# Two token halves, or two phases: the gated feed-forward of a fused two-layer kernel

## The reference

```python
def _binary_diff_weight(w, base):
    d = w - base
    coeff = jnp.mean(jnp.abs(d))
    return base + coeff * jnp.sign(d)
W1 = _binary_diff_weight(w1, mean_w1)     # (1792, 512)
W2 = _binary_diff_weight(w2, mean_w2)     # (512, 1792)
W3 = _binary_diff_weight(w3, mean_w3)     # (1792, 512)
gate = jnp.einsum('bsh,ih->bsi', hidden_states, W1)
up = jnp.einsum('bsh,ih->bsi', hidden_states, W3)
h = jax.nn.silu(gate) * up
return jnp.einsum('bsi,hi->bsh', h, W2)
```

## Time and profile before

| | us |
|---|---|
| median of three runs | 1583.92 |
| lowest, highest | 1583.92, 1591.99 |
| the profiled execution, its own time | 1585.42 |
| its span | 1583.6 |
| TensorE busy in it | 1372.1 (87%) |
| VectorE busy | 1204.4 (76%) |
| ScalarE busy | 843.5 (53%) |
| GpSimd busy | 654.1 (41%) |

### The profile page before, as it was taken

How to read it: one execution, slowest core, us unless ns; L and a number is a source line. 1 busy time by engine, 2 the same in 40 slices (tenths; PEclk the granted TensorE clock), 3 DMA queues, 4 the chain that set the end, 5 groups by cost and what they waited for, 6 DMA issues and landing times.

```text
span 1583.6 us, 21762 instructions
## 1 busy us (share of the span) xinstructions
PE 1372.1 (87%) x7310; PEld 1140.8 (72%) x7310; DVE 1204.4 (76%) x2317; ACT 843.5 (53%) x1822; POOL 654.1 (41%) x620
## 2 busy tenths in 40 slices
PE   2765999999978897888764899999999999999977
PEld 1654788788867786666443788888888888888865
DVE  6545655555545998788996898888998888898864
ACT  3675322232224565565432677766666766677741
POOL 3432000000015664564423455656555555665522
PEclk9976899999979997899756999999999999999998
DMA  6553000000021224544752000000000000000011
GB/s 220 173 161 92 0 1 1 0 1 1 1 81 47 61 84 133 155 133 152 195 173 83 13 1 26 26 26 26 26 26 26 26 26 26 26 26 14 2 72 54
DMA packets 83725, 95.62 MB, mean 60 GB/s; under 512 B 11680, under 2 KB 59296, under 8 KB 83104
## 3 DMA queue, kind: packets, MB, share of 16 engines
q1 hardware_dynamic: 83616, 94.24, 19.1%
HBM read 75.34 MB, written 18.87 MB: 59 GB/s over the span
## 4 chain that ended last, share of the span: by engine, by line
PE 66%; DVE 13%; ACT 3%; issue 2%; DMA 2%; POOL 2%; SPq 1%; DVEq 1%; POOLq 0%; ACTq 0%
PE ps L309 15%; PE ps L311 14%; PE ps L310 14%; PE ps L1545 8%; PE ps L1565 3%; PE ps L1564 3%; PE ps L1333 2%; DMA wuvo<-pr_hl 2%; DVE rop L1178 1%; DVE xn_l L1220 1%; DVE acc L1155 1%; DVE rop L1176 1%; POOL pr_hl L583 1%; PE ps L1457 1%; DVE pm L1208 1%
## 5 line engine op out<-in xcount | busy, mean ns | idle before, releaser
L644 POOL TENSOR_SCALAR pm<-pm,smx 128x128 f32<-128x128 f32 (+7 forms) x256 | 190.0, 751 | 211.8 <-DVE smx L1214 211.8
L880 ACT ACTIVATE pm<-pm,smx 128x128 f32<-128x128 f32 (+7 forms) x256 | 197.3, 772 | 35.3 <-DVE smx L1208 33.5
L1208 DVE CUSTOM_DVE_ANT_0 pm<-ps,mbias 128x128 f32<-128x128 f32 (+7 forms) x256 | 191.5, 752 | 29.1 <-PE ps L311 14.2
L1545 PE MATMUL ps<-ident,pm 128*128 128x128 f32 x1152 | 174.8, 277 | 10.1 <-DVE xn_l L1220 4.6
L886 ACT ACTIVATE xn_h<-ps 128x512 fp32r<-128x512 f32 (+3 forms) x256 | 128.5, 512 | 85.7 <-PE ps L1545 82.7
L1220 DVE TENSOR_TENSOR xn_l<-ps,xn_h 128x512 fp32r<-128x512 f32 (+3 forms) x256 | 144.5, 587 | 26.5 <-ACT xn_h L886 25.5
L309 PE MATMUL ps<-latT_l,qc_h 128*128 128x512 f32 (+3 forms) x384 | 142.7, 372 | 21.5 <-POOLq L300 12.1
L1545 PEld LDWEIGHTS ps<-ident,pm 128*128 128x128 f32 x1152 | 131.9, 141 | 36.3 <-issue 13.0
L1155 DVE SCALAR_TENSOR_TENSOR acc<-relu,iw,acc 128x768 f32<-128x768 f32 (+4 forms) x105 | 118.9, 1173 | 31.0 <-ACT relu L802 30.5
L311 PE MATMUL ps<-latT_h,qc_h 128*128 128x512 f32 (+3 forms) x384 | 134.0, 349 | 0.0
L310 PE MATMUL ps<-latT_h,qc_l 128*128 128x512 f32 (+3 forms) x384 | 133.8, 348 | 0.0
(11 more groups left out here) (246 smaller groups left out, 4009.6 us busy)
## 6 DMA issues: line engine op xcount, KB each, us to landing
iwq_raw<-in_L_attn_idx_wq_w SPq DMA_DIRECT2D x48, 256.0 KB, 3.3
ow_raw<-in_L_attn_o_w SPq DMA_DIRECT2D x16, 512.0 KB, 3.8
wuvo<-pr_hl SPq DMA_DIRECT2D x16, 512.0 KB, 3.5
base<-in_L_ffn_mean_w SPq DMA_DIRECT2D x28, 256.0 KB, 3.0
wring<-in_L_ffn_w SPq DMA_DIRECT2D x24, 256.0 KB, 3.4
wq<-pr_hl SPq DMA_DIRECT2D x16, 256.0 KB, 2.3
wuvo_h<-wuvo SPq DMA_DIRECT2D x16, 256.0 KB, 2.7
wuvo_l<-wuvo SPq DMA_DIRECT2D x16, 256.0 KB, 3.0
```

Source lines behind the costliest of these rows:

```text
L644: pool.tensor_scalar(pm[:, i % 4, 0:w], pm[:, i % 4, 0:w], smx[:, 32 + i:33 + i], 0.0, ALU.mult, ALU.add).then_inc(hd_p, 1)
L880: act.activation(pm[:, i % 4, 0:w], pm[:, i % 4, 0:w], ACT.Exp, bias=smx[:, i:i + 1], scale=-1.0, accum_out=smx[:, 16 + i:17 + i]).then_in ...
L1208: dve.tensor_tensor_reduce(out=pm[:, i % 4, 0:w], in0=two_banks(2 * (i % 2), w), in1=mbias[:, TRI[t]:TRI[t + 1]], scale=1.0, scalar=3.0 * BIG,
L1545: done = pe.transpose(ps[:, 4 + i % 2, tile(k)], pm[:, tq % 4, tile(4 * c + k)], ident[:])
```

## The change

The loop over halves goes. **Phase one** goes through the 14 chunks once: the gate for all 1024 tokens in banks 0 and 1, up in banks 2 and 3, each of the three weights transposed once, into a bank of its own (4, 5, 6). The rounded and the remainder part are made at once for gate and up only. The transposed output weight is stored unsplit in the place of its own base weight (`w2_chunk`), and silu(gate) times up in the place of the gate's and up's base weights (`h_chunk`). The output of silu goes to the free norm buffer `xn_t`. **Phase two** goes through the 14 chunks again: ScalarE and VectorE split the stored output weight and the stored product (`down_hi`, `down_lo`, two buffers), and TensorE sums the output of all eight token tiles in all eight banks, in the order `DOWN_BANKS`. At the end VectorE adds the eight banks to the residual, and then runs the statistics of all eight tiles.

The diff, cut to the lists of the three engines (the declarations of buffers and semaphores, and the old loops, are left out where they only go; the kernel before stands above):

```diff
+DOWN_BANKS = (7, 4, 5, 6, 0, 2, 1, 3)
...
-        wc_h = sbin(f_scope, "wc_h", [P, 2, 3, 512], F32R)
-        wc_l = sbin(f_scope, "wc_l", [P, 2, 3, 512], F32R)
-        silu = sbin(f_scope, "silu", [P, 512])
-        hf = sbin(f_scope, "hf", [P, 512])
-        hT_h = sbin(f_scope, "hT_h", [P, 2, 512], F32R)
-        hT_l = sbin(f_scope, "hT_l", [P, 2, 512], F32R)
+        wc_h = sbin(f_scope, "wc_h", [P, 2, 2, 512], F32R)
+        wc_l = sbin(f_scope, "wc_l", [P, 2, 2, 512], F32R)
+        w2_h = sbin(f_scope, "w2_h", [P, 2, 512], F32R)
+        w2_l = sbin(f_scope, "w2_l", [P, 2, 512], F32R)
+        hT_h = sbin(f_scope, "hT_h", [P, 2, S], F32R)
+        hT_l = sbin(f_scope, "hT_l", [P, 2, S], F32R)
...
+        def w2_chunk(g):
+            return base[2][:].rearrange("p (c n) -> p c n", c=NK)[:, :, tile(g)]
+
+        def h_chunk(g, half):
+            return base[half][:, g * 512:(g + 1) * 512]
...
+            def weight_hi(g, k):
                 act.wait_ge(ff_tr, 3 * g + k + 1)
+                act.activation(wc_h[:, g % 2, k, :], ps[:, 4 + k, :], COPY).then_inc(ff_hi, 1)
+
+            def weight_down(g):
+                act.wait_ge(ff_tr, 3 * g + 3)
+                act.activation(w2_chunk(g), ps[:, 6, :].rearrange("p (c n) -> p c n", c=NK), COPY).then_inc(ff_w2, 1)
+
+            def gate_silu(g, half):
+                act.wait_ge(ff_gate, 2 * g + half + 1)
+                reach(act, ff_mul, 2 * (g - 1) + half + 1)
+                act.activation(xn_t[:, half, :], ps[:, half, :], ACT.Silu).then_inc(ff_silu, 1)
+
+            def down_hi(g):
+                reach(act, fd_mm, g - 1)
+                act.wait_ge(ff_w2, g + 1)
+                act.activation(w2_h[:, g % 2, :].rearrange("p (c n) -> p c n", c=NK), w2_chunk(g), COPY)\
+                    .then_inc(fd_whi, 1)
+                for half in range(2):
+                    act.wait_ge(ff_mul, 2 * g + half + 1)
+                    act.activation(hT_h[:, g % 2, 512 * half:512 * half + 512], h_chunk(g, half), COPY)\
+                        .then_inc(fd_hhi, 1)
+
+            weight_hi(0, 0)
+            weight_hi(0, 1)
+            weight_down(0)
+            for g in range(NI):
+                if g + 1 < NI:
+                    weight_hi(g + 1, 0)
+                gate_silu(g, 0)
+                gate_silu(g, 1)
+                if g + 1 < NI:
+                    weight_hi(g + 1, 1)
+                    weight_down(g + 1)
+                else:
+                    down_hi(0)
+            for g in range(1, NI):
+                down_hi(g)
...
+            def weight_lo(g, k):
+                dve.wait_ge(ff_hi, 2 * g + k + 1)
+                dve.tensor_tensor(wc_l[:, g % 2, k, :], ps[:, 4 + k, :], f(wc_h[:, g % 2, k, :]),
                                   ALU.subtract).then_inc(ff_lo, 1)
...
+            def gate_mul(g, half):
+                dve.wait_ge(ff_silu, 2 * g + half + 1)
+                dve.wait_ge(ff_up, 2 * g + half + 1)
+                dve.tensor_tensor(h_chunk(g, half), ps[:, 2 + half, :], xn_t[:, half, :], ALU.mult).then_inc(ff_mul, 1)
+
+            def down_lo(g):
+                dve.wait_ge(fd_whi, g + 1)
+                dve.tensor_tensor(w2_l[:, g % 2, :].rearrange("p (c n) -> p c n", c=NK), w2_chunk(g),
+                                  f(w2_h[:, g % 2, :]).rearrange("p (c n) -> p c n", c=NK), ALU.subtract)\
+                    .then_inc(fd_w, 1)
+                for half in range(2):
+                    c = slice(512 * half, 512 * half + 512)
+                    dve.wait_ge(fd_hhi, 2 * g + half + 1)
+                    dve.tensor_tensor(hT_l[:, g % 2, c], h_chunk(g, half), f(hT_h[:, g % 2, c]), ALU.subtract)\
+                        .then_inc(fd_h, 1)
+
+            for k in range(3):
+                effective(0, k)
+            for k in range(2):
+                weight_lo(0, k)
+                effective(1, k)
+            dve.wait_ge(ff_tr, 3)
+            effective(1, 2)
+            for g in range(NI):
+                for k in range(2 if g + 1 < NI else 0):
+                    weight_lo(g + 1, k)
+                    if g + 2 < NI:
+                        effective(g + 2, k)
+                gate_mul(g, 0)
+                if g == NI - 1:
+                    down_lo(0)
+                gate_mul(g, 1)
+                if g + 2 < NI:
+                    dve.wait_ge(ff_tr, 3 * (g + 1) + 3)
+                    effective(g + 2, 2)
+            for g in range(1, NI):
+                down_lo(g)
+            for i in range(NT):
+                dve.wait_ge(ff_y, i + 1)
+                dve.tensor_tensor(xt(i), xt(i), ps[:, DOWN_BANKS[i], :], ALU.add).then_inc(ff_x, 1)
+            for t in range(NT):
+                dve.wait_ge(ff_x, t + 1)
+                dve.bn_stats(stats[:, 6 * t:6 * t + 6], xt(t))
             meet(dve, 2)
...
+            def transposes(g, k):
+                pe.wait_ge(ff_we, 3 * g + k + 1)
+                if g:
+                    if k < 2:
+                        pe.wait_ge(ff_lo, 2 * (g - 1) + k + 1)
+                    else:
+                        pe.wait_ge(ff_w2, g)
+                for c in range(NK):
+                    last = pe.transpose(ps[:, 4 + k, tile(c)], weff[:, k, tile(c)], ident[:])
+                last.then_inc(ff_tr, 1)
+
+            def project(g, k, half, done):
+                tokens = slice(512 * half, 512 * half + 512)
+                pe.wait_ge(ff_lo, 2 * g + k + 1)
+                if k == 0:
+                    reach(pe, ff_silu, 2 * (g - 1) + half + 1)
+                else:
+                    reach(pe, ff_mul, 2 * (g - 1) + half + 1)
+                for c in range(NK):
+                    last = mm3(pe, ps[:, 2 * k + half, :], wc_h[:, g % 2, k, tile(c)], wc_l[:, g % 2, k, tile(c)],
+                               xn_h[:, c, tokens], xn_l[:, c, tokens], c == 0, c == NK - 1)
+                last.then_inc(done, 1)
+
+            for k in range(3):
+                transposes(0, k)
+            for g in range(NI):
+                for k, done in ((0, ff_gate), (1, ff_up)):
+                    if g + 1 < NI:
+                        transposes(g + 1, k)
+                    for half in range(2):
+                        project(g, k, half, done)
+                if g + 1 < NI:
+                    transposes(g + 1, 2)
+
+            for g in range(NI):
+                pe.wait_ge(fd_w, g + 1)
+                for i in range(NT):
+                    if i % 4 == 0:
+                        pe.wait_ge(fd_h, 2 * g + i // 4 + 1)
+                    if g == 0:
+                        if DOWN_BANKS[i] == 6:
+                            pe.wait_ge(ff_w2, NI)
+                        elif DOWN_BANKS[i] < 4:
+                            pe.wait_ge(ff_mul, 2 * (NI - 1) + DOWN_BANKS[i] % 2 + 1)
+                    last = mm3(pe, ps[:, DOWN_BANKS[i], :], hT_h[:, g % 2, tile(i)], hT_l[:, g % 2, tile(i)],
+                               w2_h[:, g % 2, :], w2_l[:, g % 2, :], g == 0, g == NI - 1)
+                    if g == NI - 1:
+                        last.then_inc(ff_y, 1)
+                    elif i == NT - 1:
+                        last.then_inc(fd_mm, 1)
```

More of the change, by code:

```diff
@@ L275, in build @@
         wt_d, wt_abs, wt_tot = sems("wt_", "d abs tot")
-        ff_we, ff_tr, ff_hi, ff_lo = sems("ff_", "we tr hi lo")
-        ff_gate, ff_up, ff_silu, ff_mul, ff_hhi, ff_h, ff_y, ff_x = sems("ff_", "gate up silu mul hhi h y x")
+        ff_we, ff_tr, ff_hi, ff_lo, ff_w2 = sems("ff_", "we tr hi lo w2")
+        ff_gate, ff_up, ff_silu, ff_mul = sems("ff_", "gate up silu mul")
+        fd_whi, fd_w, fd_hhi, fd_h, fd_mm, ff_y, ff_x = sems("fd_", "whi w hhi h mm y x")
         lt_ld, lt_w, lt_mm, lt_ev, lt_norm, lt_tr, lt_hi, lt_lo = sems("lt_", "ld w mm ev norm tr hi lo")
@@ L732, in _ @@
             meet(act, 1)
-            def weight_hi(g, par, k):
+            def weight_hi(g, k):
                 act.wait_ge(ff_tr, 3 * g + k + 1)
[L737 to L760, removed]
@@ L909, in _ @@
         def _(dve):
-            dve.drain().then_inc(ff_lo, 2)
-            dve.drain().then_inc(ff_mul, 1)
-            dve.drain().then_inc(ff_x, 1)
             def rsqrt(k, n):
@@ L1037, in effective @@
                 dve.scalar_tensor_tensor(dst, sg, coef[:, k:k + 1], bs, ALU.mult, ALU.add).then_inc(ff_we, 1)
-            def weight_lo(g, par, k):
-                dve.wait_ge(ff_hi, 3 * g + k + 1)
-                dve.tensor_tensor(wc_l[:, par, k, :], ps[:, 6 + (3 * par + k) % 2, :], f(wc_h[:, par, k, :]),
+            def weight_lo(g, k):
+                dve.wait_ge(ff_hi, 2 * g + k + 1)
+                dve.tensor_tensor(wc_l[:, g % 2, k, :], ps[:, 4 + k, :], f(wc_h[:, g % 2, k, :]),
                                   ALU.subtract).then_inc(ff_lo, 1)
[L1044 to L1057, removed]
-                    dve.wait_ge(ff_silu, g + 1)
-                    dve.wait_ge(ff_up, g + 1)
```

(20 more changed lines are left out.)

46 lines of the change are left out of this document (removed).

## The result

The changed kernel takes 1560.82 us in the median (1557.68 to 1562.78), the kernel before 1583.92 (1581.93 to 1591.99, one more run with it). The ratio is 0.9841, 95% interval [0.9824, 0.9858]: 1.6% faster. The forecast was 1563, range 1557 to 1571. The profiled execution took 1560.82 us, its span is 1558.9 (before 1585.42 and 1583.6).

A forecast was written before the change was run, and what follows sets the result against it. The prediction took the stage to be bound by TensorE's instruction queue. Transposes 17.2, seam 5.15, output-less steps 0.5 and start 0.65 make 23.5 us gone, less 2.5 for statistics: 21.0 us, forecast 1563, own range 1558 to 1568, with C 1557 to 1571.

The forecast's parts named there:

- Item 1: Feed-forward weight transposes: 84 groups of four become 42, 13 steps' transposes at 1.32 us go, 17.2 us less.
- item 2: Seam where the two token halves meet: TensorE's gap of 5.58 us goes, 5.15 of it new.
- item 3: First output-less step of each half: gate product's wait for its one bank goes, 2 x 0.24 = 0.5 us.
- Item 4: Start of the stage: a bank for each weight lets the first product start some 0.65 us earlier, bounds nothing and 0.75.
- Phase two at 0.229 us a matmul: Phase two's 336 output matmuls: start spacing between 0.2275 and 0.2332 us, taken as 0.229; range -0.5 to +1.4 us.
- The statistics: End of the stage: all eight statistics instructions follow the last addition, four more uncovered, 2.5 us added.
- What hides: VectorE and ScalarE preparation in both phases and at the new seam runs under TensorE's matmuls and costs nothing.
- the same intervals from there to the end: Sign: behind the stage's end, near 420 us in place of 443, the program's intervals stay the same.
- C: Rival, phase one: an uncovered hand-off of about 0.5 us in each of 14 chunks, 7 us, 1570; chance 0.08.
- D: Rival: no change, as preparation paces phase one or the seam costs as much as before, 1580 to 1585; chance 0.02.
- A: Rival, phase two: operands made after the chunk before, 2.15 us 13 times, 28 us, 1591; chance 0.03.
- B: Rival, phase two: clock falls to its low level, 336 matmuls at 0.2 more, 67 us, 1630; chance 0.02.

The follow-up runs named there:

- the seam closed alone: Kernel before with its two loops over the token halves run through as 28 steps without a break, all 336 transposes kept: 1580.8 us, ratio 0.9968.
- the experiment: Changed kernel with the old waits between the first groups of transposes at the stage's start put back: 1558.77 us, stage 255.75.
- 2.4 alone: Kernel before with the first four token tiles' statistics moved behind the last addition, with the other four: 1587.59 us, ratio 1.0013.
- the first runs: Changed kernel's first measurement against the kernel before: 1560.82 us against 1583.92, ratio 0.9841.
- the second: Changed kernel measured once more, unchanged, against the kernel before: 1560.45 us, ratio 0.9839.
- The run: Changed kernel with ScalarE rounding phase two's operands only once the chunk just before is summed: 1604.43 us, ratio 1.011 to the kernel before.

## Why the prediction was right

The mechanism was the forecast's, and its own range (1558 to 1568) and the wide one held. Step by step:

- **Bound by TensorE's queue**: shown by the doubled transposes, 17.9 us in the stage with the other engines' instructions unchanged.
- **Item 1, 17.2 us**: a chunk of phase one is 12.50 us, said 12.48. Right.
- **Items 2 and 3, 5.15 and 0.5 us**: the seam closed alone, which takes item 2 and one of item 3's two places, gave 4.2, and 5.5 with the transposes that stay in that kernel, for 5.4 said. Right; the other 0.24 had no run of its own.
- **Item 4, 0.65 us**: 0.66. Right, but it was not all that the new start brings. The stage's clock rises 3.3 us sooner after the first transpose, worth 1.1 us (255.75 - 254.05, less the 0.6 of the later first product), and the experiment puts that on the breaks that the old waits made. The prediction had the low clock in its range as something that shifts by chance, and in no term.
- **Phase two at 0.229 us a matmul**: 0.2267, 0.8 us less in 336 of them. That is just below the lower bound, 0.2275, which the prediction took from an average over a whole output product.
- **The statistics, 2.5 us**: 2.5, and 2.4 alone.
- **What hides**: TensorE's list of waits names no remainder and no multiplication, only the first effective weights, 2.1 us in two places; the passage between the phases 0.24 us. VectorE's two remainders of the product ran there from 342.85 to 344.14, and the first of them, the one that the first output matmul (344.18) needs, was done some 0.7 ahead of it: the slack of 2.8 over 2.1 us, as read.

Together 25.3 and 2.5 in the stage and the gap, for 23.5 and 2.5 said: the 1.8 us are the clock at the start and the spacing in phase two. What made the rest of the median's difference, 23.1 in the first runs and 25.6 in the second, lies outside the stage and the gap and is not explained. One sign that the prediction named did not come: "the same intervals from there to the end" were 4.3 us shorter in the first profile. That is more than the 2.2 us by which the forecast missed the median, so how close the total came is in part luck; the stage and the gap are the test of the mechanism.

Of the rivals, C and D did not come. A was rightly unlikely, but wrongly priced: its waits cost the 28 us that I worked out, and its pauses 16 more, 12 of them through the clock. I had kept A and B apart, and argued from the one fall at hand, behind the 8 us of standstill in the earlier trace rows, that phase two has nothing to bring the clock down. The run shows the two together: with A, B comes too, in part. At that price A would have been well on the slower side, at 1604, and its chance belonged to slower and not to no change. The point from which it decides is lower as well: 21 us would be used up by about 1.0 us of wait a chunk, if the clock's share keeps its proportion; that is worked out, not run.

## What to carry to other kernels

Where one engine is busy for all of a stretch, count the instructions that a reordering takes out of its queue, at the distance of their starts and not at their durations; the work that goes from engines with time to spare was worth nothing here that a run could show. Then walk the two ends and the passages one by one: here they gave 6 us and took 2.5, and what was laid bare at the end could be had back by finishing the last sums at half the pace. A double buffer on TensorE's way was worth more here than the waits that it hides, 44 us for 28, because the short regular pauses cost clock as well.

## What the runs showed of the hardware

- A pause of about 2.1 us in TensorE before each chunk of 5.5 us of matmuls was enough for the clock to go down and up again in eight of 13 chunks: seven or eight matmuls 0.43 us apart each time, mean granted clock 0.89 over phase two.
- At the start of the stage, behind twelve float32 transposes without a break and four more after 0.43 us, the granted clock rose 4.9 to 5.5 us after the first transpose, in six profiles. With the same sixteen transposes broken up twice, by 0.6 to 0.7 and by 0.15 to 0.17 us, and the first product 0.6 to 0.7 us later, it rose after 8.4 to 9.0 us, in six others. With each group issued twice and no break it rose after 4.7, while transposes were all that TensorE had run in the stage.
- Float32r matmuls of 128 x 512 start 0.2333 us apart in one phase and 0.2267 in the other at the full clock, and for the first kind one bank or two in turn made no difference.
- The same code behind the stage took 1125.8 to 1133.2 us in thirteen profiles.
